# Macaron transformer, expert stages: x itself is turned, each choice gets rows of its own, and dense products fill TensorE's light stretches

## The reference

```python
xn = (x - mean) / sqrt(var + 1e-5)
x = x + 0.5 * ffn(xn)
x = x + attn(xn)
x = x + 0.5 * ffn(xn)
```

## Time and profile before

| | us |
|---|---|
| median of 3 runs | 2909.27 (2908.72 to 2911.98) |
| the profiled execution's own time | 2918.43 |
| its span | 2916.7 |
| setup | 0 to 44.8 |
| kind 0, first and second | 165.7 and 165.1 |
| kind 1, first and second | 121.0 and 120.9 |
| kind 3, first and second | 98.9 and 98.8 |
| kind 2, first and second | 26.1 and 26.4 |

### The profile page before, as it was taken

The page is one execution under the profiler, slowest core; times in us unless marked ns, Lnnn a source line. Parts: engine busy times, 40 slices in busy tenths (PEclk is TensorE's granted clock), DMA queues, the critical chain, the costliest instruction groups (busy, mean ns, idle before and its releaser), DMA issues. The chain is left out here.

```text
span 2916.7 us, 44003 instructions
## 1 busy us (share of the span) xinstructions
PE 2341.5 (80%) x13097; PEld 1224.7 (42%) x13097; DVE 2014.7 (69%) x5787; ACT 1870.3 (64%) x4763; POOL 969.9 (33%) x1288
## 2 busy tenths in 40 slices
PE   4647574828888878499999999997858888888878
PEld 4425453612222236344444444444524444444453
DVE  3605641769999956666666666665579999999855
ACT  2114323327777773467777777776549999999975
POOL 2562276254344332500000000003544444444437
PEclk8777686559999995699999999999779999999989
DMA  6330232022323200000000000000011111111000
GB/s 168 84 56 1 89 65 46 1 41 53 75 49 67 63 12 1 30 1 1 1 1 1 1 1 1 1 1 1 1 34 30 30 30 30 30 30 28 4 1 29
DMA packets 230508, 86.76 MB, mean 30 GB/s; under 512 B 175426, under 2 KB 223362, under 8 KB 230274
## 3 DMA queue, kind: packets, MB, share of 16 engines
q1 hardware_dynamic: 215168, 74.74, 11.1%
q0 software_dynamic: 9856, 7.58, 2.0%
q10 hardware_dynamic: 5250, 1.62, 0.3%
HBM read 26.47 MB, written 15.50 MB: 14 GB/s over the span
## 5 line engine op out<-in xcount | busy, mean ns | idle before, releaser
L2406 ACT ACTIVATE s_pT<-s_ps_t 128x512 f32<-128x512 f32 x1024 | 626.3, 639 | 140.4 <-PE s_ps_t L1995 124.0
L2154 DVE TENSOR_REDUCE s_neg_max<-s_ps_a 128x1 f32<-128x512 f32 x1024 | 666.8, 683 | 63.0 <-PE s_ps_a L1961 53.1
L2397 ACT ACTIVATE s_first<-s_ps_a,s_neg_max 128x512 f32<-128x512 f32 x512 | 391.5, 765 | 24.5 <-DVE s_neg_max L2154 23.0
L2007 PE MATMUL s_ps_t<-ident,s_first 128*128 128x128 f32 x2048 | 316.5, 285 | 82.0 <-ACT s_pT L2406 69.4
L2737 DVE CUSTOM_DVE_ANT_0 s_e<-s_ps_a,w_alibi 128x128 f32<-128x128 f32 (+3 forms) x512 | 231.1, 489 | 189.8 <-PE s_ps_a L2583 189.6
L2325 POOL TENSOR_SCALAR s_first<-s_first,s_rec 128x512 f32<-128x512 f32 x128 | 232.3, 1815 | 366.4 <-DVE s_rec L2160 360.4
L2853 ACT ACTIVATE s_e<-s_e,s_neg_max 128x128 f32<-128x128 f32 (+3 forms) x512 | 283.0, 555 | 43.0 <-DVE s_neg_max L2737 41.4
L1961 PE MATMUL s_ps_a<-s_lanesT 64*128 64x512 bf16 x1024 | 275.8, 401 | 37.4 <-DMA s_lanesT<-n_lanes 20.5
L2007 PEld LDWEIGHTS s_ps_t<-ident,s_first 128*128 128x128 f32 x2048 | 221.3, 142 | 181.4 <-ACT s_pT L2406 139.3
L2025 PE MATMUL s_ps_o<-s_pT,n_v_pad 128*32 128x512 f32 x2048 | 277.6, 616 | 12.2 <-ACT s_oT L2412 12.2
L2863 ACT ACTIVATE s_pT<-s_ps_t 128x512 f32<-128x512 f32 (+3 forms) x512 | 195.6, 434 | 124.1 <-PE s_ps_t L2595 123.8
(11 more groups left out here) (382 smaller groups left out, 4136.8 us busy)
## 6 DMA issues: line engine op xcount, KB each, us to landing
s_token_rows<-s_rows SPq DMA_DIRECT2D x4, 1088.0 KB, 5.4
s_x_rows<-x SPq DMA_DIRECT2D x4, 1024.0 KB, 5.3
x<-s_x_rows SPq DMA_DIRECT2D x8, 512.0 KB, 6.0
s_Wi<-L_ffn_experts_inter SPq DMA_DIRECT2D x2, 1792.0 KB, 8.1
x<-L_attn_x SPq DMA_DIRECT2D x4, 512.0 KB, 8.0
out<-x SPq DMA_DIRECT2D x8, 256.0 KB, 2.3
s_lanesT<-n_lanes SPq DMA_TRANSPOSE x64, 4.6
s_shiftedT<-n_lanes SPq DMA_TRANSPOSE x64, 2.4
```

The source lines that it names most:

```text
L2007: last = pe.transpose(st[n % NK][:, t * P:(t + 1) * P], first[:, p % NF, 2 * t + a, i * P:(i + 1) * P], G.ident[:])
L2154: dve.tensor_reduce(neg_max[:, column(n):column(n) + 1], sa[n % NA][:], AX.X, ALU.max, negate=True).then_inc(s.max_ready, 1)
L2397: act.activation(first[:, g % NF, n % PU, :], sa[n % NA][:], ACT.Exp, bias=neg_max[:, n:n + 1], accum_out=sum1[:, n % (NR * PU):n % (NR * ...
L2406: act.activation(pT[:, n % NP, :], st[n % NK][:], ACT.Exp).then_inc(s.probs_ready, 1)
```

## The change

Seven edits, given in the order of the program.

1. `stir` issues n unread bfloat16 products of 512 columns (identity times identity) into a PSUM bank that is free then: two in each round of the fronts of kinds 0, 1 and 3; eight ahead of the first expert's `turn` in kind 0; ten ahead of `turn_chosen` in kind 1, and one behind each `turn_chosen` and `take_rows`; six at the start of kind 2, and eight at the start of the attentions of kinds 1, 2 and 3.
2. Router, gate and M are multiplied by I - 1/128 in setup (`center`). The mean then drops out of every product with them, and x itself can be turned; rstd is multiplied in afterwards (the logits in kinds 0 and 3, the mask in kind 3).
3. Kind 0's front: TensorE turns x without waiting for ACT. ACT copies batch b and normalises batch b-2 behind it, and exp(0) follows the loop.
4. Kind 0's `number` works in integers (shift and mask). `told_tile` carries whether the choice is a token's second.
5. Kind 0's rows: first and second choices write to their own halves of `y_rows` (plain indirect DMA, nothing accumulates); `y_rows` is cleared by two DMAs of 2.1 MB at the start of the stage; at the end eight DMAs of 512 KB bring both halves back and eight DVE additions put them into x. `x_rows` is gone. Four gather buffers in place of three, gathers three experts ahead, marks four ahead.
6. Kind 0's `keep_own` moves from ahead of the experts to behind each `weigh` from the second on, five or six tiles at a time. Wi and Wo are loaded behind the `token_rows` stores.
7. Kind 3: x itself is turned, ACT only copies, two PSUM banks for the turned batches; DVE chooses the first half, then adds, with the second half's choosing in pieces behind pairs 0, 2, 3 and 4.

```diff
+def stir(pe, G, bank, n):
+    for _ in range(n):
+        pe.matmul(bank, G.ident16[:], G.ident16[:].unsqueeze(1).to_broadcast([P, 4, P]), start=True, stop=True)
...
+                pe.matmul(psC[:, 0:KINDS], center[:], raw_router[:], start=True, stop=True).then_inc(s.router_psum, 1)
                 multiply_linear(pe)
...
+                center_linear(pe, center)
...
+                halve_linear(dve)
+                dve.wait_ge(s.gate_psum, 1)
+                dve.tensor_copy(G.gateT[:], psC[:, 0:KINDS]).then_inc(s.gate_copied, 1)
+                copy_adapters(dve)
                 copy_linear(dve)
-                copy_adapters(dve)
...
@@ linear_experts_ffn @@
-                dve.wait_ge(s.xn_ready, NT)
-                for h in range(HALVES):
-                    choose(h)
+                shift_logits(0)
+                divide(0)
+                first_expert(0)
+                second_expert(0)
                 for t in range(0, NT, 2):
                     for e in range(E // 2):
                         add_expert(t, e)
                         add_expert(t + 1, e)
+                    if t == 0:
+                        shift_logits(1)
+                    if t == 4:
+                        divide(1)
...
-                    pe.wait_ge(s.xn_ready, TB * (b + 1))
-                    if b:
-                        pe.wait_ge(s.xnT_ready, b)
+                    if b >= 2:
+                        pe.wait_ge(s.xT_ready, b - 1)
...
@@ capacity_experts_ffn @@
-                    sp.dma_start(by_tile(x_rows)[:, half(h), :], G.x[:, half(h), :]).then_inc(s.x_stored, 16)
...
+                for n in range(2 * B // 2):
+                    c, i = n % 2, n // 2
+                    if n >= 4:
+                        sp.wait_ge(s.x_added, n - 3)
+                    sp.dma_start(parts[:, n % 4].rearrange("p (t d) -> p t d", d=D),
+                                 by_tile(y_rows[c * ROWS:(c + 1) * ROWS])[:, 2 * TB * i:2 * TB * (i + 1), :]).then_inc(loaded[n % 4], 16)
...
-                    pe.wait_ge(s.xn_ready, TB * (b + 1))
...
-                        last = pe.transpose(turned_ps[b % 2][:, t * P:(t + 1) * P], xn[:, b * TB + t, :], G.ident[:])
+                        last = pe.transpose(turned_ps[b % 2][:, t * P:(t + 1) * P], G.x[:, b * TB + t, :], G.ident[:])
...
+                    stir(pe, G, slots_ps[0][:], 2)
...
+                find_slots(2)
+                stir(pe, G, up[0][:], 8)
                 turn(0)
+                find_slots(3)
                 upward(0)
-                find_slots(2)
...
-                keep_own(0)
-                keep_own(1)
                 for e in range(E):
-                    if e + 3 < E:
-                        mark(e + 3)
-                    if e + 2 < E:
-                        read_slots(e + 2)
+                    if e + 4 < E:
+                        mark(e + 4)
                     weigh(e)
+                    if e + 4 < E:
+                        read_slots(e + 4)
+                    if e:
+                        for t in range((e - 1) * NT // (E - 1), e * NT // (E - 1)):
+                            keep_own(t)
+                for n in range(B):
+                    add_rows(n)
...
                 for b in range(B):
-                    if b + 1 < B:
-                        normalise(b + 1)
-                    if b == B - 1:
-                        exp(0)
                     copy_xnT(b)
+                    if b >= 2:
+                        normalise(b - 2)
+                exp(0)
...
-                    for q in range(Q):
-                        at = bass.IndirectOffsetOnAxis(ap=index[:, e, q:q + 1], axis=0)
-                        pool.indirect_dma_start(out=x_rows, out_offset=at, in_=y[:, e % 2, q, :], in_offset=None,
-                                                compute_op=ALU.add).then_inc(scattered[q], 16)
+                        at = bass.IndirectOffsetOnAxis(ap=to_index[:, e, q:q + 1], axis=0)
+                        pool.indirect_dma_start(out=y_rows, out_offset=at, in_=y[:, e % 2, q, :], in_offset=None
+                                                ).then_inc(scattered[q], 16)
...
@@ spline_ffn @@
+                pe.wait_ge(s.tanh_ready, 2)
+                pe.wait_ge(s.nearly_chosen, 1)
+                stir(pe, G, comp_ps[:], 10)
                 for h in range(HALVES):
                     first = h * HB
                     turn_chosen(first)
+                    stir(pe, G, comp_ps[:], 1)
                     for b in range(first + 1, first + HB):
                         turn_chosen(b)
+                        stir(pe, G, comp_ps[:], 1)
                         take_rows(b - 1)
+                        stir(pe, G, comp_ps[:], 1)
```

More of the change, by code:

```diff
@@ L227, in _ @@
                 pool.wait_ge(s.made, 2)
+                pool.tensor_scalar(center[:], G.ident[:], -1.0 / D, None, ALU.add).then_inc(s.made, 1)
+                pool.wait_ge(s.made, 3)
                 make_upto(pool)
@@ L458, in multiply, with halve, center_rows, copy @@
             last.then_inc(s.m_psum0 if e < 4 else s.m_psum1, 1)
-    def copy(dve):
+    def halve(dve):
         for i, sem in enumerate((s.m_psum0, s.m_psum1)):
             dve.wait_ge(sem, 4)
-            dve.tensor_scalar(G.M[:, 4 * i:4 * i + 4, :], ps[i][:], 0.5, None, ALU.mult).then_inc(s.m_copied, 1)
-    return s, load, multiply, copy
+            dve.tensor_scalar(M[:, 4 * i:4 * i + 4, :], ps[i][:], 0.5, None, ALU.mult).then_inc(s.m_halved, 1)
+    def center_rows(pe, center):
+        for i in range(2):
+            pe.wait_ge(s.m_halved, i + 1)
+            pe.matmul(ps[i][:], center[:], M[:, 4 * i:4 * i + 4, :], start=True, stop=True).then_inc(s.centered_psum, 1)
+    def copy(dve):
+        for i in range(2):
+            dve.wait_ge(s.centered_psum, i + 1)
+            dve.tensor_copy(G.M[:, 4 * i:4 * i + 4, :], ps[i][:]).then_inc(s.m_copied, 1)
+    return s, load, raw_gate, multiply, center_rows, halve, copy
 def linear_experts_ffn(nc, G, tag, out=None):
@@ L571, in _, with copy_xT @@
             def _(act):
[L572 to L583 removed]
+                def copy_xT(b):
+                    act.wait_ge(s.xT_psum, b + 1)
+                    act.activation(xT[:, b, :], turned[b % 2], ACT.Copy).then_inc(s.xT_ready, 1)
                 def exp(h):
@@ L596, in weigh_others @@
                                        scale=mask[:, t, E // 2 + e:E // 2 + e + 1]).then_inc(s.z_ready, 1)
-                normalise(0)
                 for b in range(B):
-                    if b + 1 < B:
-                        normalise(b + 1)
-                    copy_xnT(b)
-                for h in range(HALVES):
-                    exp(h)
+                    copy_xT(b)
+                exp(0)
                 for t in range(NT):
+                    if t == 3:
+                        exp(1)
                     weigh_others(t)
@@ L665, in make @@
         pool.wait_ge(s.upto_made, 1)
-    return s, load, make
+    return s, load, make, raw
 def capacity_experts_ffn(nc, G, inp, tag):
@@ L718, in capacity_experts_ffn @@
         slots, row, none = sb("slots", [P, 2, Q]), sb("row", [P, Q]), sb("none", [P, Q])
-        index = sb("index", [P, E, Q], I32)
+        index, to_index = (sb(n, [P, E, Q], I32) for n in ("index", "to_index"))
+        second, told_tile = sb("second", [P, NT, KINDS]), sb("told_tile", [P, NT, KINDS])
+        is_second, zeros, parts = sb("is_second", [P, Q]), sb("zeros", [P, TB * D]), sb("parts", [P, 4, TB * D * 2])
         Wi, Wo = sb("Wi", [D, E, I]), sb("Wo", [P, E, C, D])
@@ L856, in choose, with keep_own, add_rows @@
                     dve.engine_nop().then_inc(s.rows_ready, 1)
-                def keep_own(h):
-                    do(dve.tensor_copy(noop[:, half(h)], rows[:, half(h), D + E]))
-                    for t in range(h * WT, (h + 1) * WT):
-                        dve.scalar_tensor_tensor(out=G.x[:, t, :], in0=xn[:, t, :], scalar=noop[:, t:t + 1],
-                                                 in1=G.x[:, t, :], op0=ALU.mult, op1=ALU.add).then_inc(s.x_ready, 1)
+                def keep_own(t):
+                    dve.scalar_tensor_tensor(out=G.x[:, t, :], in0=xn[:, t, :], scalar=noop[:, t:t + 1],
+                                             in1=G.x[:, t, :], op0=ALU.mult, op1=ALU.add).then_inc(s.x_kept, 1)
+                def add_rows(n):
+                    i = n // 2
+                    if n == 0:
+                        dve.wait_ge(s.x_kept, NT)
+                    if n % 2:
+                        dve.wait_ge(s.x_added, n)
+                    x = G.x[:, 2 * TB * i:2 * TB * (i + 1)].rearrange("p t d -> p (t d)")
+                    dve.wait_ge(loaded[n % 4], 16 * (n // 4 + 1))
+                    dve.tensor_tensor(x, x, parts[:, n % 4], ALU.add).then_inc(s.x_added, 1)
                 def number():
```

211 lines of the change are left out of this document (125 added, 86 removed).

## The result

The changed kernel takes 2873.2 us (median of 4 runs, 2865.1 to 2887.0), the kernel before in the same comparison 2910.6 (2908.7 to 2914.9): a ratio of 0.9873, interval 0.9856 to 0.9890. It is faster by 37 us, half of the 76 forecast, and lies 1 us outside the range. Its runs spread by 22 us, those of before by 6. Which chip this first comparison ran on isn't on record.

The account below looks back on a forecast made before the run. Chains of waits were taken to bound the edited stages, with TensorE's clock low. Setup +2, kind 0 -27, kind 1 -21, kind 3 -28 and other starts -2 gave -76: 2833 us from the median, range 2800 to 2872.

Parts of the forecast that it names:

- Setup: Ahead of the stages: two centring products and a copy more, of which one product and one copy on the path, +2 us.
- Kind 0's terms: Kind 0: front -1, numbering -3, first result -6, last scatter landed 22 us earlier; with the end, -13.5 us a stage.
- the first rival: Kind 0's scatters: a plain one is as dear to issue as the adding one, POOL stays the bound; 2852 us, chance 0.15.
- the rival on the doubled rows: Kind 0's clears and doubled rows coming back cost more than they save, making the kernel slower; 2925 us, chance 0.04.
- GpSimd was not shut out by `keep_own`: Rival, kind 0's expert loop: DVE's `keep_own` stretches POOL's issues, up to 6 us a stage; 2845 us, chance 0.05.
- The step that failed in the first comparison: Kind 0's experts: results 9.45 us apart plus 3 for late marks, the seventh at 170.7 us and not 185.4.
- Kind 1: Both kind 1 stages: stirs hold the high clock in the front and the serial part from the chosen rows, -10.5 us each.
- The term that was too large: Kind 1, second half: 1.5 us more gained, since DVE's and POOL's work bounds it.
- Kind 3: Both kind 3 stages: the 9.16 us wait goes and one half's choosing leaves the path, -14 us each.
- I take it that they raise it in all three fronts: Fronts of kinds 0, 1 and 3: the stirs, two a round, raise TensorE's clock; no size of its own.
- the clock does not rise: Rival: stirs are only work; kind 0 -7, kind 1 +8, kind 3 -3 from its order; 2900 us, chance 0.08.
- the other stages: Stirs at the other starts: following TensorE work may run faster, -2 us for all five stages, between +5 and -6.

Follow-up runs that it names:

- f1: The changed kernel itself, unaltered, run again on chip D beside three variants: 2854.7 us, ratio to the kernel before 0.9776.
- e10: The changed kernel with `keep_own` back ahead of the expert loop, all 32 operations in a row: 2846.9 us, a single execution.
- A: One of the four chips of the follow-up runs; the kernel before took 2912.2 and 2913.6 us on it.
- B: Another of the four chips of the follow-up runs; the kernel before took 2911.7 us on it.
- e4: The changed kernel with three gather buffers and gathers two experts ahead, as before the change: 2874.5 us, ratio to the kernel before 0.9884.
- e6: The changed kernel with `zeros` and `parts` allocated behind kind 0's other buffers and with accumulating scatters: 2873.8 us, ratio to the kernel before 0.9862.
- f3: The changed kernel with `keep_own` alone moved back ahead of the loop, the longer lead kept, on chip D: 2863.1 us, ratio 0.9820.
- g1: The changed kernel itself a third time, on chip A: 2875.7 us, ratio to the kernel before 0.9853.
- g2: The changed kernel with three buffers, gathers two and marks three ahead, `keep_own` in the loop, on chip A: 2864.1 us, ratio 0.9822.
- e1: The changed kernel with every stir taken out, the rest as changed: 2897.3 us, ratio to the kernel before 0.9959.
- e12: The kernel before with plain scatters in place of accumulating ones, the sums left out: 2873.6 us, a single execution.
- e2: The changed kernel with scatters accumulating into the cleared rows again: 2866.0 us, ratio to the kernel before 0.9862.
- D: Another of the four chips of the follow-up runs; the kernel before took 2914.1 us on it.

## Why the prediction was half right

*Setup*: +2 was forecast, and the first stage begins at 44.6 where it began at 44.8. Between profiles this start moves by more than the term (43.8 to 46.9 in the kernels with the new setup, 42.3 and 44.8 in the two with the old), so the term is neither shown nor refuted.

*Kind 0's terms* hold where no delay comes in between. In the timeline of f1 (last weigh, last scatter, x back, last addition, next stage):

```profile
169.82 0.69 DVE L1015 TENSOR_TENSOR s_y<-s_ps_out,s_xg 128x512 f32<-128x512 f32 x1 [7.35 <-PE s_ps_out L879]
174.73 0.96 POOL L1119 DMA_INDIRECT s_y_rows<-s_y,s_to_index  x1 [0.31 <-issue]
177.07 11.43 SPq L823 DMA_DIRECT2D s_parts<-s_y_rows  x8
193.92 1.23 DVE L950 TENSOR_TENSOR x<-x,s_parts 128x1024 f32<-128x1024 f32 x1 [0.46 <-DMA s_parts<-s_y_rows]
196.28 0.87 DVE L133 BATCH_NORM_STATS2 s_stats<-x 128x6 f32<-128x128 f32 x4 [1.13 <-PEq L90]
```

The seventh result is there at 170.5 (forecast 170.7), the load starts at 177.07 (178), the next stage at 196.3 (197). A plain scatter is mostly issued in 0.97 busy and 0.30 (mean 1.05 busy with some up to 1.8; forecast 0.94 and 0.30; the earlier trace rows has 1.63 for the accumulating one), so the first rival fell. The load of `parts` takes 16.4 us, so the rival on the doubled rows fell too (its condition of 90 GB/s was also misreckoned: 4.2 MB that take 38 us longer than forecast mean some 79). GpSimd was not shut out by `keep_own`: no issue in f1 is above 1.82, whereas in e10, with the 32 operations in a row beside it, one gather took 7.91. That the end fits to 1 us is in part luck. The first gather is issued at 88.6, where I had the first index at 91.7, and `upward(0)` starts at 97.0 and not 100.5; but the first downward product stands at the low clock (5.47 and not 3.84), and from the first result to the last it is 60.8 us, not 59.7.

*The step that failed in the first comparison* is that of the experts: the first result at about 111, though `upward(0)` started early enough, and "The seventh result follows the first by 6 x 9.45 = 56.7, plus 3". TensorE's products finish late while gathers are in flight: the first result came at 117.7, 8.0 us later than in f1, and each of the next four fell 1.3 to 3.1 us further behind f1's. The last result came at 187.8 instead of 170.7, 17.1 us late, and that is the whole of +3.2 instead of -13.5 (16.7). No row of the kernel before shows it: its profile has gathers beside downward products with no waiter late. What makes the delays is not settled. Shown: they come and go with the chip, and they stay on A or B whatever is done to the stirs, the weights' load, the number of buffers, the place in SBUF, the gathers' place behind the scatters or the lead. Accumulating scatters make them smaller there. That gathers have a part in them rests on the time at which they come, since no run on A or B leaves gathers out; nor does one there have `keep_own` ahead of the loop. Whether the kernel before has them on A or B is open, since it was not profiled beside the experiments; its time there is that of the other chips, and its experts wait for POOL anyway, which could hide delays of this size.

*Kind 1*: -10.5 was forecast and -9.4 and -9.6 measured, by the named way. From the turned rows to the first use of the rows it is 8.4 us (11.8 in the earlier trace rows; forecast 8.2):

```profile
552.83 0.62 PE L1819 MATMUL s_ps_turned<-ident,s_chosen 128*64 128x128 f32 x4 [0.83 <-DVE s_chosen L1611]
561.25 0.42 DVE L1620 TENSOR_TENSOR s_u<-s_rows,s_comp 128x256 f32<-128x256 f32 x1 [6.67 <-ACT s_rows L1746]
```

From there to the last result of the half it is 14.2 us (17.8 before, forecast 14.0), and the part ahead of the turned rows gave 2.2 (forecast 1.6). The term that was too large is the second half's: 0.3 us and not 1.5.

*Kind 3*: -14 was forecast; the first stage has -14.7, by two errors that cancel. Its first addition comes 17.9 us into the stage, where I had 22.8, and the fourteen pairs behind it take 57.6 us and not 53.3. In the second stage the step "I take it that they raise it in all three fronts" failed. Here two stirs a round held a clock that was high and did not raise one that was low: the front of the last stage stayed at 0.50 with TensorE busy throughout, and in that state the stirs are only work. The rival "the clock does not rise" had the mechanism of this one stage, with -3 for its +0.4. It had kind 0's front too: where the second stage of kind 0 begins low, the first gather is issued 52.7 us into it (e4, e6, f3, g1 and g2), against 45.1 where the clock is up and 46.9 in e1, which begins low and has no stirs. So the state in which a stage begins is worth 14.6 us in the last stage (100.7 and 86.1) and about 7.6 in kind 0's second. Of sixteen profiles with the same kind 3 code, eight have the last stage low and eight high, and all three of the changed kernel itself are low. In f1's four executions the time goes with the mean clock, from 2830.8 at 0.919 to 2861.4 at 0.907, so this is probably most of their spread; only one of them was profiled.

The prediction by its parts, then, in the profiled executions: -31.5 was measured and -76 forecast. Kind 0 lost 33.4 us of the forecast gain to the delays, kind 3 lost 13.7 to the clock, kind 1 lost 2.0, and setup and the other stages gave 4.5 more than I said. f1's profile, without delays, has 34 us less in kind 0 than the first one. The fastest execution of f1 took 2830.8, where 2833 was forecast; so the forecast is about the time without delays and with the clock up, with the errors named above in it.

## What to carry to other kernels

In this kernel two unread dense products a round held a clock that was up and did not raise one that was down (0.50 for 25 us). A run of 16 raised it, in the one profile that has them; it saved 9.5 us where the clock was down and cost 3.4 where it was up, and nothing was gained in total. So look at the clock of each stage in several runs before a gain is believed.

An indirect DMA that accumulates costs POOL 1.6 us to issue where a plain one costs 1.0, and with 28 of them in a stage bound by POOL that was 19 us (e12). Two plain targets and one addition are a way to have this; the way back takes 8.8 us of it (19.2 us from the start of the load to the next stage in f1, 10.4 before). On the chips with delays the changed kernel with accumulating scatters had the shorter kind 0 stages (e2; e6's first), and no run has that variant on a chip without delays.

A kernel whose slack is taken out can be open to delays that did not show before, and these can differ between chips: repeat the kernel itself beside the variants before a cause is read from them.

## What the runs showed of the hardware that I had not expected

The same kernel took 2875.7 us on A and 2854.7 on D (medians; their ratios to the kernel before, 0.9816 to 0.9890 and 0.9727 to 0.9826, only just overlap), and 165.7 and 151.3 us in the first kind 0 stage, while the kernel before took 2911.7 to 2914.1 on all four chips. TensorE's rows can be wrong about when a product ends: by 2 to 5 us, by its waiters, while four gathers were in flight. Wide attention, whose program differs only in eight stirs at its start, took 789.4 us before and 783.2 to 789.7 in the changed kernels, 785.9 without any stir; this was not followed.
